# A longer pause on GpSimd between indirect row transfers, and one before every transfer that follows another

## What is computed

```python
x = x + _L0_attn_ref(_layernorm(x), wq, wk, wv, wo)            # 16 heads of 8, 4 key/value heads, causal
x = x + _L0_ffn_ref(_layernorm(x), router_w, router_b, w1, w2) # best 1 of 8 experts, silu-gated, 512 wide
x = x + _L1_attn_ref(_layernorm(x), W_q, W_dkv, W_uk, W_uv, W_o, ln_gamma, ln_beta) # latent keys/values, rotary
x = x + _L1_ffn_ref(_layernorm(x), gate_w, gate_b, w1, b1, w2, b2)                  # best 2 of 8, relu, 512 wide
```

## Time and profile before

| what | value |
|---|---|
| median of 3 runs | 976.34 us (975.29 to 977.66) |
| span of the profiled execution | 1059.9 us |
| its distance from the median | 83.6 us (8.6%) |
| busy in it: PE, DVE, ACT, POOL | 902.2, 667.9, 610.0, 534.5 us |
| mean granted TensorE clock | 0.922 of full speed |

### The profile page before, as it was taken

How to read it: one execution, slowest core, us unless ns; L and a number is a source line. 1 busy time by engine, 2 the same in 40 slices (tenths; PEclk the granted TensorE clock), 3 DMA queues, 4 the chain that set the end, 5 groups by cost and what they waited for, 6 DMA issues and landing times.

```text
span 1059.9 us, 25406 instructions
## 1 busy us (share of the span) xinstructions
PE 902.2 (85%) x8968; PEld 600.8 (57%) x8968; DVE 667.9 (63%) x1379; ACT 610.0 (58%) x1173; POOL 534.5 (50%) x809
## 2 busy tenths in 40 slices
PE   4699999879998999889998999978998776399791
PEld 2344554436995445349974454534447766388781
DVE  1889897857457888855669987997861351011116
ACT  3168897825445786734346867856784343155541
POOL 3144454562015776752137855676865633744442
PEclk9999999879999899789999989998988888699996
DMA  5635523353755253519844273345023445357577
GB/s 145 138 85 161 152 70 88 83 162 108 216 170 125 92 144 86 128 43 302 234 133 81 84 160 93 95 116 149 28 61 90 143 133 152 99 164 217 164 211 226
DMA packets 137317, 141.20 MB, mean 133 GB/s; under 512 B 35564, under 2 KB 113452, under 8 KB 137100
## 3 DMA queue, kind: packets, MB, share of 16 engines
q1 hardware_dynamic: 130604, 126.04, 43.7%
q0 software_dynamic: 6592, 13.55, 4.1%
HBM read 98.73 MB, written 44.36 MB: 135 GB/s over the span
## 4 chain that ended last, share of the span: by engine, by line
PE 30%; DVE 6%; another core or an unknown queue 5%; issue 5%; SPq 4%; ACT 3%; DMA 2%; POOL 0%; DVEq 0%; ACTq 0%; POOLq 0%
PE psum L1317 8%; PE psum L1327 7%; PE psum L1248 4%; DVE neg_max L1510 2%; PE psum L1204 2%; PE psum L1230 2%; SPq L963 1%; ACT scratch L1439 1%; SPq L962 1%; PE psum L1210 1%; PE psum L1274 1%; SPq L933 1%; SPq L916 1%; PE psum L1283 1%
## 5 line engine op out<-in xcount | busy, mean ns | idle before, releaser
L1510 DVE TENSOR_REDUCE neg_max<-psum 128x2 f32<-128x768 f32 (+3 forms) x352 | 380.7, 1120 | 73.2 <-PE psum L1210 52.2
L1439 ACT ACTIVATE scratch<-psum 128x1024 f32<-128x1024 f32 x320 | 316.7, 1024 | 97.2 <-PE psum L1230 84.3
L1079 POOL TENSOR_SCALAR_AFFINE_SELECT scratch<-scratch 128x512 f32<-128x512 f32 x256 | 159.0, 642 | 150.8 <-ACT scratch L1439 149.6
L1317 PE MATMUL psum<-rows_t,w_now 128*128 128x128 f32 x1360 | 177.6, 284 | 5.3 <-issue 2.2
L1248 PE MATMUL psum<-scratch,values 128*32 128x512 f32 (+3 forms) x2048 | 173.4, 460 | 1.3 <-POOL scratch L1079 0.3
L1317 PEld LDWEIGHTS psum<-rows_t,w_now 128*128 128x128 f32 x1360 | 165.6, 198 | 13.8 <-issue 8.8
L1327 PE MATMUL psum<-w,hidden_t 128*128 x992 | 140.7, 292 | 36.4 <-ACT hidden_t L1476 15.5
L1204 PE MATMUL psum<-k_stack,q_stack 52*128 52x128 bf16 (+3 forms) x1024 | 136.2, 326 | 25.7 <-DVE neg_max L1510 10.2
L1476 ACT ACTIVATE hidden_t<-psum,w_now 128x128 f32<-128x128 f32 x312 | 88.7, 372 | 115.0 <-remote 39.6
L1327 PEld LDWEIGHTS psum<-w,hidden_t 128*128 128x128 f32 x992 | 128.0, 204 | 43.4 <-issue 43.2
L1230 PE MATMUL psum<-q_stack,k_stack 55*128 55x512 bf16 (+3 forms) x1024 | 124.9, 316 | 14.5 <-DVE neg_max L1510 5.6
(11 more groups left out here) (141 smaller groups left out, 1027.5 us busy)
## 6 DMA issues: line engine op xcount, KB each, us to landing
w_now<-in_w SPq DMA_DIRECT2D x78, 322.0 KB
w_now<-in_w SPq DMA_DIRECT2D x46, 512.0 KB
q_stack<-q_parts SPq DMA_DIRECT2D x64, 192.0 KB
q_parts<-q_parts SPq DMA_DIRECT2D x16, 384.0 KB, 3.2
k_stack<-k_parts SPq DMA_DIRECT2D x32, 192.0 KB
q_parts<-q_parts SPq DMA_DIRECT2D x16, 256.0 KB, 3.0
w<-in_w SPq DMA_DIRECT2D x16, 256.0 KB, 4.5
scratch<-returned SPq DMA_DIRECT2D x16, 256.0 KB, 3.6
```

The source lines that it names most:

```text
L1079: pool.affine_select(out=diag, in_=diag, compare_op=ALU.is_ge, fill=0.0, base=0, pattern=[[0, 4], [1, P]], channel_multiplier=-1).then_inc ...
L1317: ins = pe.matmul(bank[v.bank][:, c * P:(c + 1) * P], w1_now[layer][w.slot][:, n * FFN + c * P:n * FFN + (c + 1) * P], rows)
L1439: act.activation(expd[s.slot], psum[:, u.bank:u.bank + 2, :], ACT.Exp, scale=SCALE).then_inc(read[u.bank], 1)
L1510: return dve.tensor_reduce(out=out, in_=in_, axis=AX, op=op, negate=negate)
```

## The change

The pause computes a power in place of a sum, of the same columns, and it stands in front of each indirect transfer that follows another directly, in place of each third one. Nothing else changes: order, transfers and waits of all engines are the same, and the result of the pause is still read by nobody.

```diff
--- before.py
+++ after.py
@@ -279,7 +279,7 @@
 RING_OF.update({kind: "pairs" for kind in ("max", "score", "first", "rotate_k")})
 XT_KINDS = ("turn", "turn_ctx")
 INDIRECT = ("scatter", "combine", "send")
-MOST_IN_A_ROW = 2
+MOST_IN_A_ROW = 1
 
 
 def slot_before(layer, g, x, n):
@@ -1020,7 +1020,7 @@
 
                 if pauses[0]:
                     pool.wait_ge(paused, pauses[0])
-                pool.tensor_tensor(r_small[:, 2, 0:QT], consts[:, C_EPS:C_EPS + QT], consts[:, C_HALF:C_HALF + QT], ALU.add).then_inc(paused, 1)
+                pool.tensor_tensor(r_small[:, 2, 0:QT], consts[:, C_EPS:C_EPS + QT], consts[:, C_HALF:C_HALF + QT], ALU.pow).then_inc(paused, 1)
                 pauses[0] += 1
 
             for s in plan.order("pool"):
```

## The result

The changed kernel takes **1069.76 us** (median of 4 runs, 1067.96 to 1073.11); the kernel before takes 975.92 us beside it (975.29 to 977.66). The ratio is 1.0968, 95% interval 1.0936 to 1.1000: 9.7% slower, 93.8 us. The forecast was 1019 us in a range of 979 to 1042. The sign was right. The forecast growth, 43 us, was under half of that, and the time lies outside the range.

The account below looks back on a forecast made before the run. TensorE set the pace at the end; with the change GpSimd's transfers would. Last stage 31, clock 7, fetch 4 and masks 1 gave 43 us on 976.3: 1019 us, range 979 to 1042.

Parts of the forecast that it names:

- Rival (c): At GpSimd's transfers: the pause is nearly free, time stays at 976 us, give or take 4; chance 0.09.
- Rival (a): TensorE's hold-ups are in timed runs too and stay: last send +4.6, masks +6, 982 us; chance 0.17.
- Rival (b): Spacing transfers ends real TensorE hold-ups: -7.0 in the last stage, about -10 in all, 966 us; chance 0.12.
- The masks that stand behind a pair of scatters or gathers: Attention masks on GpSimd: 0.9 to 2 us later each time, mostly covered by idle time; +1 (0 to 6).
- the fetch: SyncE's fetch of sorted rows behind the first 16 scatters: they end 10.4 us later; +4 us (0 to 7).
- the clean length of the last stage: End of layer 1 without stops: last send starts at 1002.2 us before, 1033.3 after, +31 us.
- the 38.1 us of stops: TensorE standing still eight times at the end of layer 1, read as caused by profiling and subtracted.
- the clock term: TensorE's matmuls at half clock in the last stage's profile, taken as slower than timed runs: +7 us (0 to 17).
- the pace, 2.20 us: Each paused transfer on GpSimd: 0.98 + 0.03 + 1.03 + 0.16 = 2.20 us, 1.33 before.
- 2.20 us for a send is more than the 1.78 us in which TensorE finishes a slot: Last stage: from the first send on, GpSimd can't keep up with TensorE's expert slots.
- part of the 40 us not named: Span-to-runs difference outside the named hold-ups; part may lie in the last stage, so range some 10 us wider above.
- the 83.6 us: Profiled span of 1059.9 us less the 976.34 us median; about half ascribed to hold-ups caused by profiling.

Follow-up runs that it names:

- e5: The change only in layer 1's scatters behind its first group and the sends, old pauses elsewhere: 1072.14 us, ratio 1.0084 to the kernel before at 1064.80 us.
- e4: The change everywhere except layer 1's scatters behind its first group and the sends, which keep the old pause: 1012.48 us, ratio 1.0372 to the kernel before.
- e7: The change only in the 32 scatters of layer 1's first group: 1060.17 us, ratio 0.9950 to the kernel before at 1064.80 us.
- e8: The change only in the first 16 scatters of layer 0: 1063.14 us, ratio 0.9998 to the kernel before at 1064.80 us.
- e10: Power of two columns before each transfer of the last stage only, old pause elsewhere: 1000.12 us, ratio 1.0252 to the kernel before.
- e3: Kernel before with its 62 pauses kept in place, each a power in place of the sum: 991.59 us, ratio 1.0159 to the kernel before.
- e6: The changed kernel with a power of two columns in place of four: 1027.57 us, ratio 0.9651 to the kernel before at 1064.80 us.
- e9: Kernel before with no pause at all: 975.46 us, ratio 0.9983 to the kernel before at 977.8 us.
- s5: Same edit as e6, two-column power everywhere, on another chip: 1022.32 us, ratio 1.0476 to the kernel before.

## Why the prediction was wrong

**The sign, and what bounds the end: right.** GpSimd's chain of transfers sets the end, at 2.305 us a transfer, with "issue" ahead of each. GpSimd's share of the last chain is 32% (0% before, at least 10% forecast); its busy time is 691.8 us (680 forecast). TensorE's last expert product starts at 1012.21 us, 37 us ahead of the last send; before it was 2.2. What lies behind the last send is 19.6 us, 19 forecast. Rival (c), a pause that overlaps, is refuted by the timeline: 1.04 us each, in full. Rival (a) is refuted where the time is 976 us, as there are no hold-ups to stay. Rival (b) has the mechanism right on the chip of 1065 us, but its -7 us for the last stage rests on 2.20 us a transfer; with 2.305 the stage grows there too (`e5`).

**The step that failed first: "The masks that stand behind a pair of scatters or gathers come 0.9 to 2 us later each time; their idle time covers most of it, and I take +1 (0 to 6)", with "the fetch", +4.** Both together were 5 us, and at most 13. Measured are 33 us by the traces and 36.9 by `e4`. The delay itself was worked out rightly: 10.4 us at the 16th scatter forecast, 10.3 measured. I followed it only to SyncE's fetch, and did not ask who waits for the five masks that stand next in GpSimd's string. The 150.8 us of idle time in front of masks are a sum over 256 of them; a mask that follows a burst of transfers has none of it, and TensorE came for it 1.5 us after GpSimd had begun it (231.45 and 230.00 us), which leaves no room for 10.3. The delays also do not end with the burst: the table has them grow from 10 to 14.6, 22 and 33 us. Of these 33, 21 are TensorE's idle time and 12 its longer busy time (the windows above).

**The second: the clean length of the last stage.** Taking the 38.1 us of stops out of the profile was right for these runs, but the reason, "the likeliest reading is that profiling causes them", was wrong; they are the stops that `e7` and `e8` show on a chip on which the timed runs are slow as well. The subtraction left 205 us for the stage (797.2 to 1002.2). It is 193.4. That is 12 us, of which the 7 of the clock term were meant to pay a part. Against the second profile, the stage of the first is 49.7 us longer (243.1 and 193.4): TensorE's waits of over 1.2 us come to 42.5 us in place of 12.8, and it is busy for 186.9 us in place of 169.2 with the same work, at a granted clock of 0.88 in place of 0.96. So 30 us were stops, since a part of such waits is there in every run, and the slower work, put at 7 (0 to 17), was 18. The window of the stage in the first profile:

```profile
797.19:1040.27 243.08, 186.91 (x1378) 173.54 (x1376) 48.13 (x219) 101.40 (x338) 118.02 (x165) 0.88 0.54 157
```

**The third: the pace, 2.20 us.** The sum was the right one, with each part a little short: the power 1.046 for 1.03, the transfer behind a power 1.03 for 0.98, the gaps 0.20 for 0.16. The interval is 2.305, and 106 times 0.105 is 11 us. With both, the stage grows by 55 us and not by 31 + 7: 236 + 11 = 247 with the measured pace, where 248.8 was measured, against 193.4.

**A reason that was right in its outcome only: "2.20 us for a send is more than the 1.78 us in which TensorE finishes a slot".** In the last 30 transfers the kernel before itself needs 67.4 us, 2.32 each, as TensorE is busy for 58.1 of them, with rows to turn besides the slots, and waits in the rest; there GpSimd at 2.305 keeps up. The loss is made earlier. In the first 78 intervals before needs 126.0 us, 1.61 each, and the changed kernel 181.5, 2.33 each: 55.5 us more, the whole of it. Of the first 79 transfers 30 are scatters, for which TensorE has no slot to compute, and which the comparison of one send with one slot left out: the 49 sends alone come every 2.6 us before. Of the 55.5 TensorE loses 19 itself, since the scatters of the later groups come late: layer 1's first product at L1327 is 35.4 us late, that of 24 slots later 54.1. The wait of 13.2 us at L1299 is most of it, and the changed kernel's VectorE shows what it hangs on:

```profile
875.11 0.17 DVE L1532 TENSOR_SCALAR xn_half<-xn_half 128x4 f32<-128x4 f32 x1 [15.10 <-DMA sorted_in<-xn_half,rows_of]
```

The marking stands in VectorE's order in front of results that TensorE needs, and waits for first scatters that GpSimd issues only up to 872.74 us. The kernel before, run again, has the last two such marks at 820.36 and 835.96 with no wait of VectorE; there it is GpSimd that waits for the marks. The other 35 us remain as sends that are still to be done when TensorE has finished. With a pace of 1.99 or 1.81 to 2.04 (`e10`, `e3`) a part of the backlog is worked off again at the end: `e3` is 18.0 us late at transfer 79 and 9.9 at the last send.

The sum of the terms as measured: 12.0 for the first 16 scatters, 13.0 for the 32 of layer 1, some 12 for the other scatters and the gathers, 55.0 in the last stage, 92 in all, against 93.8 (and 92.7 in the second measurement). The 12 are what `e4` leaves over; the check that the sum passes is that of its two halves, 36.9 and 55.0.

**Why the range failed.** The upper bound took 10 us for "part of the 40 us not named", and the masks at 6 at most. No row bounded the masks from above. A bound was in the order of the steps: TensorE's values products wait for all that GpSimd is late by, less the room between a mask and its product.

**The gap between span and runs.** The Trainium skill (Runtime: NRT & Kernel Launch, the breakdown of preamble and postamble) has 6.2 us between a profile's total and the execution time. In every execution here whose own time is known the two are 1.8 us apart (1068.8 and 1070.62; 980.4 and 982.22). Size and sign differ: here the time is the longer one, and the span goes only from the first to the last instruction, so the total of the Trainium skill and this span may not be the same thing. What holds is that the distance is small and the same in every execution, and I should have taken the 83.6 us as a sign that the profile and the runs were of different kinds. The warning of the Trainium skill on dense semaphore increments (VectorE: DVE Perf Modes, the section on the TRN2 errata) fits the one chip in its direction: there signals between engines come up to 20 us late beside transfers in close succession, and `e6`, which spaces them, gains 37 us. On one of the other chips `e9`, with no pause at all, is no slower. The Trainium skill speaks there of a deadlock, which no run here shows.

## What to carry to other kernels

Idle time summed over a group is no cover for a burst: look at the very instruction that stands behind the burst in the engine's order, and at who waits for it. An engine that gets a fixed addition to every step has to be set against the consumer's pace stretch by stretch; where it is slower than the densest stretch (1.61 us here) a backlog arises, and it goes away only if a later stretch is slower than the new pace. Compare the span of a profile with the runs before using it, and take a second profile if they are a few per cent apart: the row that looks like a bottleneck may be that of another chip. A row "another core or an unknown queue" in the chain of a program on one core was the sign of it here. And follow a wait back until you come to an engine that waited for nothing, or to a signal that nothing in the program explains.

## What was not expected of the hardware

- The kernel before takes 975.5 to 977.8 us on three chips and 1064.8 us on a fourth, and there alone, and in the first profile, this kernel's TensorE stands still for up to 10.7 us beside indirect transfers in close succession (`e8`), while VectorE and ScalarE wait for signals that come 9 and 20 us behind the products (the first profile, 903.97 to 913.25 and 905.27 to 925.30 us). The kernel with a rest of 0.73 us in front of every transfer hardly knows the difference (`e6` and `s5`, 1027.6 and 1022.3 us). So the same pause is worth -3.5% on one chip and +4.8% on another.
- A power on GpSimd takes 1.046 us for four columns and 0.732 for two: by estimate 0.157 us a column and 0.42 fixed, if it is linear, while the sum of four takes 0.21.
- An indirect transfer that follows a power takes 1.03 us, one that follows a transfer 0.96 and one behind a sum 1.00.
